# A decoder layer on one core: weight splits, scores, copies and stores of the context attention in another order

## What is computed

```python
x = layernorm(x + local_attention(x))      # 16 heads, 17 neighbours, learned soft window
x = layernorm(x + xattn(x, ctx, ctx))      # causal: scores / 16, softmax, times ctx
x = layernorm(x + ffn(x))                  # top 2 of 8 experts: gelu(x @ w1[e].T) @ w2[e].T, gated
```

## Time and profile before

| | us |
|---|---|
| median of 3 runs | 1128.37 |
| lowest, highest | 1128.18, 1131.3 |
| the profiled execution | 1127.54 |
| its span | 1125.7 |

### The profile page before, as it was taken

One profiled execution on the slowest core, in us unless ns is written; L12 is line 12 of the kernel. 1 busy time (PEld: TensorE's weight loads), 2 busy tenths in 40 slices (PEclk: granted clock), 3 DMA queues, 4 the chain that ended last, 5 costly groups with the idle time before them and its releaser, 6 DMA issues.

```text
span 1125.7 us, 25018 instructions
## 1 busy us (share of the span) xinstructions
PE 952.7 (85%) x8131; PEld 768.9 (68%) x8132; DVE 797.3 (71%) x1147; ACT 486.4 (43%) x1149; POOL 725.3 (64%) x469
## 2 busy tenths in 40 slices
PE   9993199989989989787877579999999999999960
PEld 5552198978978978665656467777777777777740
DVE  5889999999999998558888854454445445444435
ACT  3697434445545554345665413233223223322325
POOL 4687999999999999401000346666666666667532
PEclk9997599999999999899999689999999999999985
DMA  3271212221221221487765512222222222222227
GB/s 107 70 138 27 65 29 66 70 70 47 70 65 51 70 62 55 185 301 252 232 215 169 174 39 40 47 42 44 45 46 43 42 47 42 45 44 42 33 30 298
DMA packets 69916, 100.24 MB, mean 89 GB/s; under 512 B 9248, under 2 KB 51680, under 8 KB 68928
## 3 DMA queue, kind: packets, MB, share of 16 engines
q1 hardware_dynamic: 53968, 81.04, 22.7%
q0 software_dynamic: 15904, 18.66, 10.6%
HBM read 73.82 MB, written 26.25 MB: 89 GB/s over the span
## 4 chain that ended last, share of the span: by engine, by line
PE 44%; POOL 19%; issue 17%; DVE 10%; ACT 5%; DMA 3%; POOLq 0%; SPq 0%; DVEq 0%; ACTq 0%
PE psum L797 18%; PE psum L805 11%; POOL mid L1270 10%; PE psum L807 5%; POOL arena L1275 2%; DVE arena L1634 2%; PE psum L600 2%; POOL arena L1261 2%; PE psum L684 2%; POOL arena L1281 2%; PE psum L789 1%; ACT arena L1181 1%; PE psum L733 1%; POOL arena L1224 1%; DMA sum_dram<-arena,mid 1%
## 5 line engine op out<-in xcount | busy, mean ns | idle before, releaser
L797 PEld LDWEIGHTS psum<-arena 128*128 x3408 | 239.0, 98 | 75.2 <-issue 8.8
L797 PE MATMUL psum<-arena 128*128 128x128 f16 x3408 | 286.7, 220 | 4.1 <-DVE arena L1790 1.6
L620 PE MATMUL psum<-consts,mid 128*128 128x128 f32 x2108 | 245.1, 277 | 43.9 <-POOL mid L1270 43.9
L620 PEld LDWEIGHTS psum<-consts,mid 128*128 128x128 f32 x2108 | 240.1, 193 | 53.7 <-issue 40.2
L1270 POOL TENSOR_TENSOR mid<-arena 128x2304 f32<-128x2304 f32 (+1 forms) x62 | 251.3, 4075 | 9.4 <-POOL arena L1261 7.6
L805 PE MATMUL psum<-arena 128*128 x568 | 215.0, 380 | 4.9 <-DVE arena L1781 1.2
L1349 POOL DMA_INDIRECT sum_dram<-arena,mid x71 | 141.8, 1997 | 43.6 <-issue 19.5
L1790 DVE SCALAR_TENSOR_TENSOR arena<-psum,arena 128x256 f32<-128x256 f32 x71 | 34.3, 484 | 186.1 <-ACT arena L1153 110.9
L1153 ACT ACTIVATE arena<-psum,arena 128x256 f32<-128x256 f32 x71 | 33.6, 473 | 296.4 <-PE psum L807 296.4
L1473 DVE TENSOR_REDUCE arena<-mid 128x272 f32<-128x4624 f32 x32 | 158.9, 4965 | 1.7 <-ACT mid L954 1.4
L807 PE MATMUL psum<-arena 128*128 x568 | 154.8, 273 | 0.0
(11 more groups left out here) (198 smaller groups left out, 1477.7 us busy)
## 6 DMA issues: line engine op xcount, KB each, us to landing
arena<-w_t SPq DMA_DIRECT2D x64, 256.0 KB, 2.8
arena<-w_t SPq DMA_DIRECT2D x16, 1024.0 KB, 10.3
arena<-x SPq DMA_DIRECT2D x32, 128.0 KB, 2.1
arena<-x_dram SPq DMA_DIRECT2D x8, 512.0 KB, 5.2
arena<-ctx_t SPq DMA_DIRECT2D x8, 512.0 KB, 6.0
arena<-ctx SPq DMA_DIRECT2D x8, 512.0 KB, 6.7
x_dram<-mid SPq DMA_DIRECT2D x8, 512.0 KB, 3.3
arena<-sum_dram SPq DMA_DIRECT2D x8, 512.0 KB, 7.5
```

What stands on the lines that cost most here:

```text
L620: last = nc.tensor.matmul(psum[:, u, c * P:(c + 1) * P], av_prod[half][:, w, c * P:(c + 1) * P], ident, start=(a + w == 0 and c == 0), sto ...
L797: last = nc.tensor.matmul(dst, block_of(w, e, 0, c * F + j * P, P), x[:, u, c * P:(c + 1) * P], start=(k == 0 and c == 0), stop=(k == 2 an ...
```

## The change

In `attend` ScalarE makes all four high parts behind exponentials and copies instead of two ahead of them, and exp(0) ahead of `x2_transposed`; TensorE makes all four scores ahead of `transpose_x2`; VectorE makes its first three low parts behind sums 0, 1 and 2. In the last windows TensorE adds x to window 29 behind both halves of sum 30. SP stores x1's first two parts during the windows, loads sequence 0's ctx during window 31, and stores the last part in two: sequence 0's 16 partitions ahead of the load of its rows, the others behind it. Low_part(7, 1, 0) moves ahead of the wait for the routing product, and TensorE waits for the low parts at its second lot.

```diff
             def load_x_res(t, u, i):
+                load_w_piece(t)
+                load_x(t, u, i)
+            steps(sp, CHUNK - 8, load_x_res)
+            load_w_piece(CHUNK - 8)
+            store_x1(0)
+            load_x(CHUNK - 8, 0, CHUNK // 2 - 4)
+            load_x_res(CHUNK - 7, 1, CHUNK // 2 - 4)
+            steps(sp, CHUNK - 2, load_x_res, CHUNK - 4, CHUNK - 6)
+            load_w_piece(CHUNK - 2)
+            store_x1(1)
+            load_x(CHUNK - 2, 0, CHUNK // 2 - 1)
+            load_w_piece(CHUNK - 1)
+            sp.wait_ge(penalties_laid, 2 * CHUNK)
+            load_ctx(0, 0)
+            load_x(CHUNK - 1, 1, CHUNK // 2 - 1)
+            for part in (2, 3):
+                store_x1(part)
+            a, z = PARTS[4]
+            sp.wait_ge(x1_last, z - (CHUNK - LAG))
+            sp.dma_start(x1_chunk[0:PER, a:z, :], q_all[0:PER, a:z, :]).then_inc(first_stored, 16)
...
-                    sp.wait_ge(x1_stored, 16 * len(PARTS))
+                    sp.wait_ge(first_stored, 16)
+                    sp.wait_ge(x1_stored, 16 * (len(PARTS) if past(b, 1) else 4))
                 sp.dma_start(x1_n[:, u], x1_seq[bass.ds(b, 1)].rearrange(rows_of, p=P)).then_inc(x1_loaded[u], 16)
+                if not past(b, 1):
+                    sp.dma_start(x1_chunk[PER:, a:z, :], q_all[PER:, a:z, :]).then_inc(x1_stored, 16)
+                if past(b, 1):
+                    load_ctx(b, u)
...
-            sum_window(CHUNK - 2, 0, 0)
+            for half in range(2):
+                sum_window(CHUNK - 2, 0, half)
             add_x(CHUNK - 3, 1, CHUNK // 2 - 2)
-            sum_window(CHUNK - 2, 0, 1)
...
                     last.then_inc(s_done, 1)
-                    if t == QT - 2 and past(b, 1):
-                        transpose_x2(b - 1, 1 - u)
                 if past(b, 1):
+                    transpose_x2(b - 1, 1 - u)
                     route(b - 1)
...
-            pe.wait_ge(w_low_made, 4 * N_EXP)
...
                 if e_up is not None:
+                    if not past(s, 2):
+                        pe.wait_ge(w_low_made, 4 * N_EXP)
                     pe.wait_ge(rows_low, s)
...
-                if past(b, 1):
-                    high_parts(b - 1, 0)
...
                 if past(b, 1):
                     keep_x2(b - 1, 1 - u)
+                exp(0)
+                if past(b, 1):
                     x2_transposed(b - 1)
-                exp(0)
                 exp(1)
+                if past(b, 1):
+                    high_part(b - 1, 0, 0)
                 copy(0)
                 exp(2)
                 copy(1)
                 exp(3)
                 copy(2)
                 if past(b, 1):
-                    high_part(b - 1, 1, 0)
+                    high_part(b - 1, 0, 1)
                 copy(3)
                 if past(b, 1):
-                    high_part(b - 1, 1, 1)
+                    high_part(b - 1, 1, 0)
                 if more:
                     copy_x1t(b + 1)
+                if past(b, 1):
+                    high_part(b - 1, 1, 1)
...
                 scale_peaks(0)
-                if past(b, 1):
-                    low_part(b - 1, 0, 0)
                 mask(3)
...
-                    if t == 0 and past(b, 1):
-                        low_part(b - 1, 0, 1)
-                    if t == 1 and past(b, 1):
+                    if t < 2 and past(b, 1):
+                        low_part(b - 1, 0, t)
+                    if t == 2 and past(b, 1):
                         low_part(b - 1, 1, 0)
...
+            low_part(N_EXP - 1, 1, 0)
             dve.wait_ge(routing_products, 3)
...
             nc.vector.tensor_copy(slot_word, word_sum).then_inc(past_made, 1)
-            low_part(N_EXP - 1, 1, 0)
             low_part(N_EXP - 1, 1, 1)
```

More of the change, by code:

```diff
@@ L378, in decoder_layer @@
         x1_stored = sem("x1_stored")
+        first_stored = sem("first_stored")
         prob_made = sem("prob_made")
@@ L516, in _, with load_w_piece @@
             sp.wait_ge(gate_arg, 2 * GATE_PARTS)
-            def load_x_res(t, u, i):
+            def load_w_piece(t):
                 if past(t, 1):
@@ L523, in load_x_res, with load_x @@
                     sp.dma_start(w_piece[:, k, :], parts[bass.ds(t, 1)].rearrange("a p x -> p (a x)")).then_inc(w_piece_loaded, 16)
+            def load_x(t, u, i):
                 if past(t, 2):
@@ L526, in load_x_res, with store_x1 @@
                 sp.dma_start(x_res[:, u, :], x_chunk[:, bass.ds(t, 1), :].rearrange("p a e -> p (a e)")).then_inc(x_res_loaded[u], 16)
-            steps(sp, CHUNK, load_x_res)
-            for a, z in PARTS:
+            def store_x1(part):
+                a, z = PARTS[part]
                 sp.wait_ge(x1_ready, min(z, CHUNK - LAG))
@@ L533, in _, with load_ctx, load_x_res @@
                 sp.dma_start(x1_chunk[:, a:z, :], q_all[:, a:z, :]).then_inc(x1_stored, 16)
+            def load_ctx(b, u):
+                rows_of = "a (t p) e -> p (a t) e"
+                sp.dma_start(ctx_ts[:, u], ctx_t[bass.ds(b, 1)].rearrange("a (c p) l -> p (a c) l", p=P)).then_inc(ctx_loaded[u], 16)
+                sp.dma_start(ctx_sb[:, u], ctx[bass.ds(b, 1)].rearrange(rows_of, p=P)).then_inc(ctx_loaded[u], 16)
+            def load_x_res(t, u, i):
+                load_w_piece(t)
[18 more added lines that the diff above has]
+            sp.dma_start(x1_chunk[0:PER, a:z, :], q_all[0:PER, a:z, :]).then_inc(first_stored, 16)
             def load_sequence(b, u, i):
@@ L541, in load_sequence @@
                 else:
-                    sp.wait_ge(x1_stored, 16 * len(PARTS))
+                    sp.wait_ge(first_stored, 16)
+                    sp.wait_ge(x1_stored, 16 * (len(PARTS) if past(b, 1) else 4))
                 sp.dma_start(x1_n[:, u], x1_seq[bass.ds(b, 1)].rearrange(rows_of, p=P)).then_inc(x1_loaded[u], 16)
-                sp.dma_start(ctx_ts[:, u], ctx_t[bass.ds(b, 1)].rearrange("a (c p) l -> p (a c) l", p=P)).then_inc(ctx_loaded[u], 16)
-                sp.dma_start(ctx_sb[:, u], ctx[bass.ds(b, 1)].rearrange(rows_of, p=P)).then_inc(ctx_loaded[u], 16)
+                if not past(b, 1):
+                    sp.dma_start(x1_chunk[PER:, a:z, :], q_all[PER:, a:z, :]).then_inc(x1_stored, 16)
+                if past(b, 1):
+                    load_ctx(b, u)
                 for k, (w, x) in enumerate(((w1_t, F), (w2_t, E))):
```

## The result

The changed kernel takes 1136.36 us in the median (1134.71 to 1136.71, 4 runs) beside 1128.28 for the kernel before (1127.9 to 1131.3, 4 runs). The comparison's ratio is 1.0063, with a 95% interval of 1.0043 to 1.0083: slower, and above the range forecast. The profiled execution took 1136.69 us, its span 1134.8, against 1125.7 before: 9.1 us more.

| stretch | before | after | change | forecast |
|---|---|---|---|---|
| start to the close of sequence 0 | 497.01 | 496.55 | -0.5 | -2.0 |
| from there to the close of sequence 7 | 122.89 | 134.40 | **+11.5** | +7.2 |
| from there to the first product of the experts | 42.41 | 40.11 | -2.3 | -2.6 |
| from there to the end | 463.39 | 463.74 | +0.3 | 0 |

The account below looks back on a forecast made before the run. In attend no engine is full; each sequence is a chain of handovers, its second half on VectorE. 7.2 - 0.6 - 1.4 - 2.6 = +2.6 us gave 1130.1 profiled, 1130.9 median; range 1128.2 to 1133.4.

Parts of the forecast that it names:

- Part 1: Attend's sequences 1 to 7: a third low part behind each router product, slightly earlier routers in most; +7.2 us together.
- R to V: From the router product's end to the sequence's close, VectorE's stretch of the chain; forecast +7.5 us over seven sequences.
- V to R: From a close to the next router product's end; forecast -0.3 us: +0.9 in sequence 1, -0.2 in the others.
- Part 2: Last windows: sum 30 no longer waits behind add_x(29), so the mixed rows' copy starts earlier; -0.6 us.
- Part 3: Entry to the context stage: scores start at 481.0, held by the fillers and no longer by ctx; -1.4 us.
- Part 4: Ahead of the experts: one low part fills VectorE's wait and TensorE turns lot 0 earlier; -2.6 us.
- A: Rival, attend's sequences: VectorE swallows the third low part in waits; faster, -6.0 us, 1122.4; chance 0.10.
- B: Rival, ScalarE in attend: exp(0) ahead of x2_transposed holds the turned rows; slower, +3.5 us, 1134.4; chance 0.13.
- C: Rival, the last store of x1: splitting it saves nothing; 1131.3 us; chance 0.10.
- D: Rival, ahead of the experts: the gather of lots 0 and 1 ends last, losing 1.3 us; 1132.2; chance 0.07.

Follow-up runs that it names:

- e2: The changed kernel with five fillers on TensorE between the turned rows and the router product; 1130.15 us.
- e8: e2 with high_part(0,0) back ahead of keep_x2 and low_part(0,0) back in its old place ahead of mask(3); 1125.62 us.
- e1: The changed kernel with TensorE's, ScalarE's and VectorE's orders in attend put back; windows, stores, ctx load and tail stay changed; 1123.40 us.
- e5: The changed kernel with ScalarE's and VectorE's orders in attend put back, TensorE's new order kept, no fillers; 1126.46 us.
- e6: e1 with ScalarE's copy(3) ahead of high_part(1,0), and VectorE's low_part(1,0) behind sum 2 instead of sum 1; 1118.33 us.
- e3: The kernel before with only the three new orders in attend; 1141.49 us.
- e10: e1 with low_part(7,1,0) back behind past_made and TensorE waiting for all low parts ahead of lot 0; 1124.66 us.
- e9: e1 with the last part of x1 stored whole, in one transfer ahead of the load of x1_n; 1123.06 us.
- e7: e6 with all scores ahead of the turned rows, five fillers ahead of the router product, and x2_transposed ahead of keep_x2; 1121.09 us.
- e4: The changed kernel with only TensorE's order in attend put back (turned rows between scores 2 and 3); 1138.54 us.
- e11: e1 with add_x(29) back between the halves of sum 30; 1123.65 us.

## Why the prediction was wrong

**The orders (Part 1): right in mechanism and size, where the clock holds.** Behind the router R to V cost +8.2, forecast +7.5, and +7.54 with the fillers (e2). The third low part is the cause (e8: 6.3 of it back). The wait for high_part(1,0) stayed at 0.5 us as worked out, and sequences 6 and 7 lost 0.9 each there in e2 (9.41 and 9.40 to 10.30 and 10.31), as forecast.

**The step that failed** is the one on V to R: "So the transposes start where they did. [...] Gain 0.2 to 0.3; I take 0.2". It took TensorE's durations, measured at a granted clock of 1.00, over to an order in which TensorE sits idle for ScalarE's copy and then runs products of 8 columns, and priced the gap as idle time of an engine that nobody waits for. The router product, on the chain, then took 2.74 instead of 1.95 us in the worst looped sequences, and the V to R of all seven came out at +3.3 instead of -0.3: 3.6 us, of which the fillers gave back 3.3. No rival named the clock, though the earlier trace rows showed it at 0.50 in the fillers for five us, behind 3.85 us without TensorE.

**Part 2: -1.2 from the start of the sum to the store, forecast -0.6.** ScalarE's copy of the mixed rows starts 461.60 - 451.62 = 9.98 us behind the sum's start, where I had worked out 461.7 - 451.26 = 10.4, and the 0.2 kept for meeting silu_y was not needed. The sum itself started 0.4 us later in this execution, so 0.9 of it shows at the store.

**Part 3: right start, wrong speed.** The scores began at 480.91 as forecast, but by another way and so with luck: the fillers ended at 477.7, forecast 479.1, and x1_n held the transposes until 478.93. Their price (4.58 in the trace of before) failed as Part 1's did: 6.23, three of the six us at half clock. The code ahead of them doesn't decide it: they took 4.55 in e1, e2, e5 and e6, and 6.26 in e3, which has the code of the kernel before ahead of them. **Part 4** gave 2.3 in the change and 2.5 alone (e10), forecast 2.6.

**The rivals.** A (VectorE swallows the third low part) falls with e8. B: exp(0) began 0.97 us behind keep_x2, as soon as the next could in the earlier trace rows, and held nothing: x2_transposed ended at 578.97, 2.4 us behind the turned rows' start, before 2.5 (552.97 to 555.49). C holds in its effect on the kernel's time (e9), not in its premise: the split store did not take as long as the whole one. From its issue to the load that it released, it took 1.61 to 1.81 us in eight of the ten profiled executions that have it and 3.54 and 3.56 in the change and e1; the whole one took 4.27 before, 4.07 in e3 and 2.37 in e9. The rule cited with it (the Trainium skill, DMA: Bandwidth & Descriptors, Rules for kernel authors: two transfers to disjoint partitions are not worth making) agrees with e9 as far as the kernel's time goes, where the fillers cover the store; on a store whose first part alone is waited for, these durations neither bear it out nor refute it. D was not seen: lot 0 was turned at 668.82, right behind past_made. The chance of "slower", given as 0.36, adds up to 0.40 from its own terms (0.18, 0.13, 0.05 and 0.035); nothing else hangs on it.

**The sum by what was measured:** orders 7.5, clock in the sequences 4.0, the stages around them -4.9, the slow first scores 1.7: +8.3, beside +8.1 between the medians.

What stays open: why the first scores ran at half clock in the change and e3 and not in e2, and why e7's first sequence is long behind the router.

## What to carry to other kernels

An engine whose clock depends on its own work is not free to idle: before taking the product that fills TensorE's wait to another place, ask what runs in the gap instead, and price everything behind it on the chain at both clock levels. If the order must have the gap, a few useless products that fit inside it are cheaper (4.0 us back here). And moving work "behind" something only helps when the place that it leaves was not a free hole: low_part(0,0) cost nothing where it was, and 6.2 us in seven sequences where it went.

## What the runs showed that I had not expected

- The granted clock fell to 0.50 where TensorE had been idle for only 1.35 us (577.7 to 579.0) and then ran sixteen products of 8 columns, and came back after 6.6 us of work. The length of the gap alone does not decide it. In the same run, behind gaps of 1.22 us (554.22 to 573.09) and 1.32 us (592.74 to 611.02), the router product kept its 1.95 us and the clock fell only behind it (0.50 from 562.9 and from 600.5 on). In e4 it fell around gaps of 2.45 to 2.72 us ahead of the turned rows (1.97 us instead of 1.09), but not around one of 2.48 in sequence 2; and in e6 gaps of 1.40 to 1.70 us at the same place left it at 1.00.
- Where the clock falls counts as much as whether it does: behind the router product it cost nothing with three low parts there (e2), and with two anything from nothing to 0.8 us a sequence (R to V 9.71 us in sequence 5 of e9, 9.88 in sequence 2 of e1 and 10.19 in sequence 6 of e8, beside 9.70, 9.74 and 9.41 before).
- The fillers ahead of the stage ran 6.57 to 8.08 us for the same 44 products; in e6 (6.58) and e1 (8.08) nothing ahead of them differs. They run at 0.50 until the clock comes back. The start of the scores moves with it: 8.4 us behind the last store in e6 (478.86 - 470.42), 9.9 in e1 (481.60 - 471.66).
- From the last store's issue to the load that it released: 1.62 us in e2, e6 and e11, 1.81 in e10, 3.56 in e1 for the same 32 KB; 2.37 in e9, 4.07 in e3 and 4.27 before for 256 KB. With 2 us between equal transfers, one profiled execution can't price one.
